# The head of a residual projection kernel: a weight loaded in three transfers, GpSimd adding the identity, products and a bias copy reordered

## The chip, the core and the metric

The kernel runs on one core of one Trainium2 chip. The metric is the device time of one execution in microseconds. A separate profiled execution gives the trace.

## What is computed

`x` is 128 x 128 x 512 in fp32, `cond` 128 x 512. With the 1024 x 512 `weight_matrix` cut into halves W_u and W_e:

```python
u = jax.nn.gelu(encoded_utterance @ W_proj + b_proj, approximate=False)
W_u, W_e = (weight_matrix[:D], weight_matrix[D:])
logits = (u @ W_u)[:, None, :] + jnp.einsum('bnd,dc->bnc', element_embeddings, W_e)
return x + logits
```

Here `encoded_utterance` is `cond` and `element_embeddings` is `x`. So the output is x (W_e + I) plus a bias row for each b, and the kernel computes it in that form.

## The kernel before

**The arithmetic.** Every fp32 operand is split into a high part (cast to the type fp32r) and a low part (the rest); a product is three matmul passes, high by high, high by low and low by high. W_e lies as `w_e[p, j, c]` in four slices j of 512 columns; the identity is added on a diagonal of each slice, then the slice is cast into `w_hi[j]` and the rest goes into `w_lo[j]`.

**The stages.** The first four of the 128 n ("direct" chunks 0 and 1, two n each) are multiplied plainly: TensorE transposes x (`flip`), ACT casts the high part (`direct_hi`), DVE makes the low part (`split_direct`), and TensorE multiplies (L688 for chunk 0, L726 to L728 for chunk 1). The other 124 n go in 31 quads of four n. In each quad the work is a 2 x 2 block scheme with seven products `m1` to `m7` instead of eight, 12 matmuls each (L743 to L747, `three_passes`), whose operands are blocks of x and their sums (`s1` to `s4`), and blocks of the weight and their sums (`t_sum`, `t_hi`, `t_lo`). DVE transposes the quad (`turn_up`, `turn_low`, L509) and forms `s1` (L552), `s3` (L558), `s2` (L564) and the low part of `s1` (L567); ACT casts the high parts (L391, L399), copies snapshots of partial sums between banks (L452, L461) and seeds banks with the bias (L424, L432); GpSimd makes the other low parts and `s4`. In a period k the products of quad k run while quad k+1 is prepared.

**The bias.** TensorE transposes `cond` (L673), multiplies with W_proj (L717), transposes again, ACT applies the GELU (L382), TensorE multiplies with W_u (L735) between the two halves of chunk 1's products, and DVE copies the sum to `bias` (L635) and makes `bias_step` (L637). ACT's `seed_a` (L424) waits for `bias_step`; `m1(0)` waits for the seed. `evacuate(c)` (L513) on DVE adds the bias to the direct chunks.

**Order.** Each engine has its own queue, in the order of the program, and semaphores between them. Around the change:

- SP issues all transfers: `load_direct(0)`, the two halves of W_e (L245, slices 0 and 1, then 2 and 3), `load_direct(1)`, `cond`, W_proj, b_proj, W_u, then the first quad in two halves (`load_first`, L232) and the next ones (L237).
- DVE: add the identity to slice 0, cast `w_hi[0]` (L608), `split_direct(0)`, add 1, `split_direct(1)`, add 2, add 3 (all L593), the four `split_w` (L602), four `t_sum`, `split_direct` of chunk 1, the transposes of quad 0, `sum_s1`, `sum_s2`, `split_s1`, `sum_s3`, bias copy, `bias_step`, `evacuate(0)`, `evacuate(1)`, the transposes of quad 1, and then, in `period(0)`, `combine_quad(1)`, which begins with `sum_s1(1)`.
- ACT: `direct_hi` of chunk 0, `w_hi[1]` to `w_hi[3]` (L364), chunk 1's, `t_hi` and `cond_t`, then for quad 0 `up`, `hi_s1`, `hi_a22`, `hi_s2`, `hi_s3`, `seed_a`, `seed_c`, `hi_s4`; in period 0 the bank copy L444, `seed_c(1)`, `up(1)`, `snap5` (L452), `seed_a(1)`, `hi_s1(1)`, `snap2` (L461).
- TensorE: six dummy matmuls on zeros, the transposes of chunk 0, eight more dummies (`WARM_ON`, L669), and then for each j: high products of slice j (two matmuls), low products of slice j, and the products with `w_lo[j-1]`; the transposes of chunk 1 stand at j = 2, that of `cond` at j = 3.
- GpSimd: the identity matrix, the four low parts of `t_sum` (L308), then quad work.

`m7(0)` waits for `snap2` (L461), `m5(0)` for `s1_lo` and `seed_c(0)`.

Of the kernel before, what the change touches and what calls it, by code (L numbers as in the profile page):

```python
# [8 lines left out]
ALU = mybir.AluOpType  # L9
# [6 lines left out]
HEAD_CHUNKS = 2  # L16
QUAD = 4
WARM_UP = 6
WARM_ON = 8


def build_cond_residual(nc, x, cond, weight_matrix, w_proj, b_proj, out):
# [18 lines left out]
    NJ = D // P  # L41
    NM = B // Q
    T = TILES_PER_CHUNK
# [13 lines left out]
    with ExitStack() as ctx:  # L57
# [3 lines left out]
        def sem(name):  # L61
            return ctx.enter_context(nc.semaphore(name))
# [76 lines left out]
        cond_loaded = sem("cond_loaded")  # L139
        w_proj_loaded = sem("w_proj_loaded")  # L140
        b_proj_loaded = sem("b_proj_loaded")
        w_e_loaded = [sem(f"w_e_loaded{n}") for n in range(2)]
        direct_loaded = [sem(f"direct_loaded{c}") for c in range(HEAD_CHUNKS)]
        direct_flipped = sem("direct_flipped")
        direct_hi_ready = sem("direct_hi_ready")
# [14 lines left out]
        bias_copied = sem("bias_copied")  # L160
        bias_ready = sem("bias_ready")
        w_diag_ready = sem("w_diag_ready")
        w_hi_ready = [sem(f"w_hi_ready{j}") for j in range(NJ)]
        w_lo_ready = [sem(f"w_lo_ready{j}") for j in range(NJ)]
        t_summed = sem("t_summed")
# [54 lines left out]
        def first_half(n):  # L220

            return quad_raw[0][:, n * T * TILE:(n + 1) * T * TILE].rearrange("p (m n w) -> p m n w", m=NM, n=T)

        def stores_before(k, p):

            return (k + p) * 8

        @block.sync
        def _(sp):
# [11 lines left out]
                sp.dma_start(direct[:, c * T:(c + 1) * T, :],  # L241
                             x[:, c * T:(c + 1) * T, :]).then_inc(direct_loaded[c], 16)

            def load_w_e(n):
                sp.dma_start(w_e[:, 2 * n:2 * n + 2, :], w_e_dram[:, 2 * n:2 * n + 2, :]).then_inc(w_e_loaded[n], 16)  # L245

            load_direct(0)
            for n in range(2):
                load_w_e(n)
            load_direct(1)  # L250
            sp.dma_start(cond_sb[:, :], cond).then_inc(cond_loaded, 16)
            sp.dma_start(w_proj_sb[:, :, :], w_proj_dram).then_inc(w_proj_loaded, 16)
# [31 lines left out]
            n = N - QUAD  # L284
# [14 lines left out]
        @block.gpsimd  # L299
        def _(pool):  # L300
            pool.memset(ident[:, :], 0.0).then_inc(ident_zeroed, 1)
            pool.wait_ge(ident_zeroed, 1)
            pool.affine_select(out=ident[:, :], in_=ident[:, :], compare_op=ALU.not_equal, fill=1.0,
                               base=0, pattern=[[-1, P]], channel_multiplier=1).then_inc(ident_ready, 1)

            def split_t(n):
                pool.wait_ge(t_hi_ready, n + 1)
                pool.tensor_tensor(t_lo[:, n, :, :], t_sum[:, n, :, :], t_hi[:, n, :, :].bitcast(F32),  # L308
                                   ALU.subtract).then_inc(t_lo_ready, 1)

            for n in range(4):
                split_t(n)

            def prepare(k, p, first=False):
                pool.wait_ge(up_hi, k + 1)
                pool.tensor_tensor(slot(lo[p], UP, 2), a_up[p], slot(hi[p], UP, 2).bitcast(F32),  # L316
                                   ALU.subtract).then_inc(up_lo, 1)

                def sum_s4():
                    pool.wait_ge(s2_ready, k + 1)  # L320
                    pool.tensor_tensor(s4[p], a12[p], s2[p], ALU.subtract).then_inc(s4_ready, 1)  # L321

                def split_s2():
                    pool.wait_ge(s2_hi, k + 1)
                    pool.tensor_tensor(slot(lo[p], S2), s2[p], slot(hi[p], S2).bitcast(F32),  # L325
                                       ALU.subtract).then_inc(s2_lo, 1)

                if first:
                    split_s2()
                    sum_s4()  # L330
                else:
                    sum_s4()
                    split_s2()
                pool.wait_ge(s4_hi, k + 1)
                pool.tensor_tensor(slot(lo[p], S4), s4[p], slot(hi[p], S4).bitcast(F32),  # L335
                                   ALU.subtract).then_inc(s4_lo, 1)
                pool.wait_ge(s3_hi, k + 1)
                pool.tensor_tensor(slot(lo[p], S3), s3[p], slot(hi[p], S3).bitcast(F32),
                                   ALU.subtract).then_inc(s3_lo, 1)
                pool.wait_ge(a22_hi, k + 1)  # L340
                pool.tensor_tensor(slot(lo[p], A22), a22[p], slot(hi[p], A22).bitcast(F32),  # L341
                                   ALU.subtract).then_inc(a22_lo, 1)

            prepare(0, 0, True)
            prepare(1, 1)
            with pool.Fori(1, QUADS // 2) as it:
                for p in range(2):
                    prepare(it * 2 + p, p)
            prepare(QUADS - 1, 0)

        @block.scalar
        def _(act):
# [7 lines left out]
            for n in range(T):  # L360
                direct_hi(n)
            for j in range(1, NJ):
                act.wait_ge(w_diag_ready, j + 1)
                act.copy(w_hi[:, j, :], w_e[:, j, :]).then_inc(w_hi_ready[j], 1)  # L364
            for n in range(T, HEAD):
                direct_hi(n)
# [140 lines left out]
        def _(dve):  # L507
# [79 lines left out]

            dve.memset(zeros[:, :], 0.0).then_inc(zeros_ready, 1)

            def add_identity(j):  # L590
                dve.wait_ge(w_e_loaded[j // 2], 16)
                diag = w_e[:, j, :].rearrange("p (a r) -> p a r", r=NJ)[:, :, j]
                dve.tensor_tensor(diag, diag, ident[:, :], ALU.add).then_inc(w_diag_ready, 1)  # L593

            def split_direct(n):
                dve.wait_ge(direct_hi_ready, n + 1)
                dve.tensor_tensor(x_lo[n // T][:, n % T, :, :], direct_psum[n % T],
# [5 lines left out]
                                  ALU.subtract).then_inc(w_lo_ready[j], 1)  # L603

            dve.wait_ge(ident_ready, 1)
            add_identity(0)
            dve.wait_ge(w_diag_ready, 1)
            dve.tensor_copy(w_hi[:, 0, :], w_e[:, 0, :]).then_inc(w_hi_ready[0], 1)  # L608
            split_direct(0)
            add_identity(1)  # L610
            split_direct(1)
            add_identity(2)
            add_identity(3)
            for j in range(NJ):
                split_w(j)

            b_of = w_e[:, :, :].rearrange("p (e j) (h c) -> p e h j c", e=2, h=2)
            b11, b12, b21, b22 = b_of[:, 0, 0], b_of[:, 0, 1], b_of[:, 1, 0], b_of[:, 1, 1]
            dve.wait_ge(w_diag_ready, NJ)
            dve.tensor_tensor(t_sum[:, 0, :, :], b12, b11, ALU.subtract).then_inc(t_summed, 1)  # L620
            dve.tensor_tensor(t_sum[:, 2, :, :], b22, b12, ALU.subtract).then_inc(t_summed, 1)
            dve.wait_ge(t_summed, 1)
# [5 lines left out]
            turn_up(0, 0, True)  # L628
            turn_low(0, 0, True)
            sum_s1(0, 0, True)  # L630
            sum_s2(0, 0)
            split_s1(0, 0)
            sum_s3(0, 0, True)
            dve.wait_ge(bias_summed, 1)
            dve.tensor_copy(bias[:, :], bias_psum).then_inc(bias_copied, 1)  # L635
            dve.wait_ge(bias_copied, 1)
            dve.tensor_tensor(bias_step[:, :], bias_psum[:, right], bias[:, left], ALU.subtract).then_inc(bias_ready, 1)  # L637
            evacuate(0)
            evacuate(1)
            turn_up(1, 1, True)  # L640
# [25 lines left out]
        def _(pe):  # L666
# [20 lines left out]
            def product(t, a, b, j, first=False, last=False):  # L687
                return pe.matmul(banks[0][:, t, :], a[:, t, j, :], b[:, j, :], start=first, stop=last)  # L688

            for j in range(NJ + 1):  # L690
                if j < NJ:
                    pe.wait_ge(w_hi_ready[j], 1)
                    for t in range(T):
                        if j == 0:
                            pe.wait_ge(direct_hi_ready, t + 1)
                        product(t, x_hi[0], w_hi, j, first=(j == 0))
                    for t in range(T):
                        if j == 0:
                            pe.wait_ge(direct_lo_ready, t + 1)
                        product(t, x_lo[0], w_hi, j)  # L700
# [149 lines left out]
```

## Time and profile before

| | us |
|---|---|
| median of 3 runs | 347.29 (346.6 to 347.96) |
| the profiled execution | 347.7 |
| its span, first to last instruction | 345.4 |
| TensorE busy with matmuls | 339.6 (98%) |
| DVE / ACT / GpSimd busy | 261.7 / 247.0 / 277.2 |

The span is what the instructions cover; 2.3 us of the execution's time lie around it. All rows below are from the profiled execution, and their times count from the start of its span. In a row, an engine's name with a q is its queue (SPq issues transfers). A matmul's duration includes its way through the array; start to start is what the next one waits.

### The profile page before, as it was taken

How to read it: one execution, taken by the hardware profiler on the slowest of the kernel's cores; microseconds unless marked ns; L12 is line 12 of the kernel's file. 1: busy time of each engine (PE TensorE's matmuls, PEld its weight loads, DVE VectorE, ACT ScalarE, POOL GpSimd, SP SyncE). 2: the span in 40 equal slices, each digit the busy share in tenths (PEclk: the TensorE clock that was granted, in tenths of full speed). 3: DMA queues.
4: the chain of work that ended last, by engine and by line, in shares of the span. 5: the costliest groups of instructions: out<-in, count | busy, mean ns of one | idle time of the engine just before them, and what ended most of it. 6: DMA issues, size and time to landing. Idle time of an engine off the chain costs nothing.

```text
span 345.4 us, 7856 instructions
## 1 busy us (share of the span) xinstructions
PE 339.6 (98%) x2706; PEld 328.7 (95%) x2706; DVE 261.7 (76%) x301; ACT 247.0 (72%) x424; POOL 277.2 (80%) x196
## 2 busy tenths in 40 slices
PE   7999999999999999999999999999999999999996
PEld 3758999999999999999999999999999999999996
DVE  2869977788777778877777897777789777778811
ACT  3646877877777787777778777777877777787741
POOL 0357998888989888898988889898888989888860
PEclk9999999999999999999999999999999999999999
DMA  7998697888799788879978887997887799788116
GB/s 257 331 180 236 123 238 201 221 194 204 176 228 241 195 219 196 198 180 229 237 200 218 195 197 178 232 233 202 219 197 197 175 235 237 197 209 210 83 56 228
DMA packets 72264, 70.64 MB, mean 205 GB/s; under 512 B 2880, under 2 KB 67392, under 8 KB 68032
## 3 DMA queue, kind: packets, MB, share of 16 engines
q1 hardware_dynamic: 72256, 70.53, 80.5%
q8 instruction: 5, 0.08, 0.1%
q14 instruction: 3, 0.02, 0.0%
HBM read 36.96 MB, written 33.55 MB: 204 GB/s over the span
## 4 chain that ended last, share of the span: by engine, by line
PE 89%; DVE 1%; ACT 0%; issue 0%
PE banks L743 30%; PE banks L747 29%; PE banks L745 29%; DVE work L509 1%; DVE banks L509 0%; DVE banks L552 0%; ACT snap_rows L461 0%; ACT y L504 0%; ACT hi L399 0%
## 5 line engine op out<-in xcount | busy, mean ns | idle before, releaser
L743 PE MATMUL banks<-t_hi,hi 128*128 128x256 f32 x496 | 140.5, 283 | 0.2 <-ACT snap_rows L461 0.2
L745 PE MATMUL banks<-t_lo,hi 128*128 128x256 f32 x496 | 140.4, 283 | 0.0
L747 PE MATMUL banks<-t_hi,lo 128*128 128x256 f32 x496 | 140.4, 283 | 0.0
L743 PE MATMUL banks<-w_hi,hi 128*128 128x256 f32 x372 | 105.3, 283 | 0.4 <-ACT banks L424 0.4
L745 PE MATMUL banks<-w_lo,hi 128*128 128x256 f32 x372 | 105.3, 283 | 0.0
L747 PE MATMUL banks<-w_hi,lo 128*128 128x256 f32 x372 | 105.3, 283 | 0.0
L509 DVE STREAM_TRANSPOSE work<-quad_raw 128x1024 f32<-128x1024 f32 (+1 forms) x62 | 100.7, 1624 | 3.6 <-DMA quad_raw<-in_x 3.6
L743 PEld LDWEIGHTS banks<-t_hi,hi 128*128 128x128 f32 x496 | 95.2, 192 | 0.6 <-issue 0.6
L747 PEld LDWEIGHTS banks<-t_hi,lo 128*128 128x128 f32 x496 | 95.2, 192 | 0.0
L745 PEld LDWEIGHTS banks<-t_lo,hi 128*128 128x128 f32 x496 | 95.2, 192 | 0.0
L316 POOL TENSOR_TENSOR lo<-work,hi 128x1024 fp32r<-128x1024 f32 x31 | 74.8, 2413 | 21.7 <-ACT hi L391 21.7
L399 ACT CAST hi<-work 128x512 fp32r<-128x512 f32 x124 | 71.0, 619 | 16.1 <-DVE work L564 8.4
L743 PEld LDWEIGHTS banks<-w_hi,hi 128*128 128x128 f32 x372 | 71.4, 192 | 0.8 <-issue 0.8
L747 PEld LDWEIGHTS banks<-w_hi,lo 128*128 128x128 f32 x372 | 71.4, 192 | 0.0
L745 PEld LDWEIGHTS banks<-w_lo,hi 128*128 128x128 f32 x372 | 71.4, 192 | 0.0
L321 POOL TENSOR_TENSOR work<-work 128x512 f32<-128x512 f32 x31 | 40.3, 1299 | 18.8 <-DVE work L564 18.8
L581 DVE TENSOR_TENSOR y<-banks,snap_rows 128x512 f32<-128x512 f32 x31 | 21.4, 691 | 36.2 <-PE banks L747 36.2
L444 ACT COPY banks<-banks 128x512 f32<-128x512 f32 x30 | 17.1, 570 | 44.4 <-PE banks L747 44.3
L586 DVE TENSOR_TENSOR y<-banks,snap_rows 128x512 f32<-128x512 f32 x31 | 21.4, 692 | 27.2 <-PE banks L747 27.2
L325 POOL TENSOR_TENSOR lo<-work,hi 128x512 fp32r<-128x512 f32 x31 | 40.5, 1305 | 1.4 <-ACT hi L399 1.4
L335 POOL TENSOR_TENSOR lo<-work,hi 128x512 fp32r<-128x512 f32 x31 | 40.4, 1302 | 1.4 <-ACT hi L399 1.4
L341 POOL TENSOR_TENSOR lo<-work,hi 128x512 fp32r<-128x512 f32 x31 | 40.6, 1310 | 0.0
(71 smaller groups left out, 401.7 us busy)
## 6 DMA issues: line engine op xcount, KB each, us to landing
out<-y SPq DMA_DIRECT2D x31, 1024.0 KB, 4.5
quad_raw<-in_x SPq DMA_DIRECT2D x120, 256.0 KB, 5.7
head_raw<-in_x SPq DMA_DIRECT2D x2, 512.0 KB, 5.7
w_e<-in_L_cond_weight_matrix SPq DMA_DIRECT2D x2, 512.0 KB, 6.2
w_proj_sb<-in_L_cond_W_proj SPq DMA_DIRECT2D x1, 1024.0 KB, 10.0
w_u<-in_L_cond_weight_matrix SPq DMA_DIRECT2D x1, 1024.0 KB, 12.3
quad_raw<-in_x SPq DMA_DIRECT2D x8, 128.0 KB, 9.5
out<-y SPq DMA_DIRECT2D x3, 256.0 KB, 2.1
```

Source lines behind the costliest of these rows:

```text
L316: pool.tensor_tensor(slot(lo[p], UP, 2), a_up[p], slot(hi[p], UP, 2).bitcast(F32), ALU.subtract).then_inc(up_lo, 1)
L321: pool.tensor_tensor(s4[p], a12[p], s2[p], ALU.subtract).then_inc(s4_ready, 1)
L325: pool.tensor_tensor(slot(lo[p], S2), s2[p], slot(hi[p], S2).bitcast(F32), ALU.subtract).then_inc(s2_lo, 1)
L335: pool.tensor_tensor(slot(lo[p], S4), s4[p], slot(hi[p], S4).bitcast(F32), ALU.subtract).then_inc(s4_lo, 1)
L341: pool.tensor_tensor(slot(lo[p], A22), a22[p], slot(hi[p], A22).bitcast(F32), ALU.subtract).then_inc(a22_lo, 1)
L399: act.copy(slot(hi[p], at), source).then_inc(done, 1)
L509: return dve.transpose(out_, in_)
L581: dve.tensor_tensor(y[p][:, upper, right], c_bank[p], snap2[p][:, :, :], ALU.add).then_inc(c12_out, 1)
L586: dve.tensor_tensor(y[p][:, lower, right], a_bank[p], snap5[p][:, :, :], ALU.add).then_inc(c22_out, 1)
L743: pe.matmul(psum[:, t, :], a_hi[:, 2 * j + t, :], b_hi[:, j, :], start=False, stop=False, skip_group_check=True)
L745: pe.matmul(psum[:, t, :], a_hi[:, 2 * j + t, :], b_lo[:, j, :], start=False, stop=False, skip_group_check=True)
L747: last = pe.matmul(psum[:, t, :], a_lo[:, 2 * j + t, :], b_hi[:, j, :], start=False, stop=(j == T - 1), skip_group_check=True)
```

## The change

W_e is loaded in three transfers instead of two: slice 0, slice 1, slices 2 and 3. DVE adds the identity to slice 0 only; GpSimd, behind its identity matrix, does so for slices 1 to 3. ACT's casts wait for GpSimd. TensorE runs six dummies instead of eight behind the first transposes, and then takes the high products of slice j+1 ahead of the low products of slice j. On DVE `sum_s3(0)` stands ahead of `sum_s2(0)`, and the bias copy and `bias_step` stand ahead of `split_s1(0)`.

```diff
-WARM_ON = 8
+WARM_ON = 6
...
-            def load_w_e(n):
-                sp.dma_start(w_e[:, 2 * n:2 * n + 2, :], w_e_dram[:, 2 * n:2 * n + 2, :]).then_inc(w_e_loaded[n], 16)
+            def load_w_e(n, js):
+                sp.dma_start(w_e[:, js, :], w_e_dram[:, js, :]).then_inc(w_e_loaded[n], 16)
 
             load_direct(0)
-            for n in range(2):
-                load_w_e(n)
+            load_w_e(0, slice(0, 1))
+            load_w_e(1, slice(1, 2))
+            load_w_e(2, slice(2, NJ))
             load_direct(1)
...
+            pool.wait_ge(ident_ready, 1)
+            for j in range(1, NJ):
+                pool.wait_ge(w_e_loaded[min(j, 2)], 16)
+                diag = diagonal(j)
+                pool.tensor_tensor(diag, diag, ident[:, :], ALU.add).then_inc(w_diag_ready, 1)
...
             for j in range(1, NJ):
-                act.wait_ge(w_diag_ready, j + 1)
+                act.wait_ge(w_diag_ready, j)
                 act.copy(w_hi[:, j, :], w_e[:, j, :]).then_inc(w_hi_ready[j], 1)
...
             dve.wait_ge(ident_ready, 1)
-            add_identity(0)
-            dve.wait_ge(w_diag_ready, 1)
+            dve.wait_ge(w_e_loaded[0], 16)
+            first_diag = diagonal(0)
+            dve.tensor_tensor(first_diag, first_diag, ident[:, :], ALU.add).then_inc(first_diag_ready, 1)
+            dve.wait_ge(first_diag_ready, 1)
             dve.tensor_copy(w_hi[:, 0, :], w_e[:, 0, :]).then_inc(w_hi_ready[0], 1)
             split_direct(0)
-            add_identity(1)
             split_direct(1)
-            add_identity(2)
-            add_identity(3)
             for j in range(NJ):
                 split_w(j)
...
             sum_s1(0, 0, True)
+            sum_s3(0, 0, True)
             sum_s2(0, 0)
-            split_s1(0, 0)
-            sum_s3(0, 0, True)
             dve.wait_ge(bias_summed, 1)
             dve.tensor_copy(bias[:, :], bias_psum).then_inc(bias_copied, 1)
             dve.wait_ge(bias_copied, 1)
             dve.tensor_tensor(bias_step[:, :], bias_psum[:, right], bias[:, left], ALU.subtract).then_inc(bias_ready, 1)
+            split_s1(0, 0)
             evacuate(0)
...
+            def high(j):
+                pe.wait_ge(w_hi_ready[j], 1)
+                for t in range(T):
+                    if j == 0:
+                        pe.wait_ge(direct_hi_ready, t + 1)
+                    product(t, x_hi[0], w_hi, j, first=(j == 0))
+
+
+            high(0)
             for j in range(NJ + 1):
+                if j + 1 < NJ:
+                    high(j + 1)
                 if j < NJ:
-                    pe.wait_ge(w_hi_ready[j], 1)
-                    for t in range(T):
-                        if j == 0:
-                            pe.wait_ge(direct_hi_ready, t + 1)
-                        product(t, x_hi[0], w_hi, j, first=(j == 0))
                     for t in range(T):
```

`diagonal(j)` is the view of slice j on which the identity is added, 128 elements a partition with a step of four.

## Rows read from the trace of the kernel before

**Rows 1.** Windows: busy time (x instructions) of each engine, PEclk, DMA share, GB/s.

```profile
36.70:342.70 306.00, 305.74 (x2544) 305.36 (x2544) 236.27 (x267) 227.84 (x390) 260.27 (x180) 1.00 0.80 201
```

**Rows 2.** Chain of waits, 18 to 37 us: start, us, what; one link.

```profile
35.96 0.60 ACT snap_rows L461
```

**Rows 3.** Timeline, TensorE, 22 to 37 us: start, us, line, tiles, count, idle before.

```profile
22.23 3.67 PE L735 MATMUL banks<-w_u,u_t 128*128 128x512 f32 x8
...
28.27 0.39 PE L728 MATMUL banks<-w_hi,lo 128*128 128x512 f32 x1
29.11 0.36 PE L743 MATMUL banks<-w_hi,hi 128*128 128x256 f32 x1 [0.45 <-ACT banks L424]
...
36.26 0.28 PE L747 MATMUL banks<-w_hi,lo 128*128 128x256 f32 x1
36.70 0.36 PE L743 MATMUL banks<-t_hi,hi 128*128 128x256 f32 x1 [0.16 <-ACT snap_rows L461]
```

**Rows 4.** Timeline, DVE, 21 to 31 us.

```profile
21.72 1.21 DVE L509 STREAM_TRANSPOSE banks<-quad_raw 128x512 f32<-128x512 f32 x1 [0.32 <-DMA quad_raw<-in_x]
...
24.05 0.70 DVE L552 TENSOR_TENSOR banks<-banks,work 128x512 f32<-128x512 f32 x1
25.40 0.69 DVE L564 TENSOR_TENSOR work<-banks,work 128x512 f32<-128x512 f32 x1 [0.65 <-ACT hi L399]
...
26.60 0.68 DVE L558 TENSOR_TENSOR work<-work,banks 128x512 f32<-128x512 f32 x1
27.20 0.68 DVE L635 COPY bias<-banks 128x512 f32<-128x512 f32 x1
27.92 0.42 DVE L637 TENSOR_TENSOR bias_step<-banks,bias 128x256 f32<-128x256 f32 x1
28.26 2.35 DVE L513 TENSOR_TENSOR y<-banks,bias 128x1024 f32<-128x1024 f32 x2
30.52 2.10 DVE L509 STREAM_TRANSPOSE work<-quad_raw 128x1024 f32<-128x1024 f32 x1
```

**Rows 5.** Timeline, ACT, 24 to 29 us: casts of s1 and s3, seed.

```profile
24.78 0.59 ACT L399 CAST hi<-banks 128x512 fp32r<-128x512 f32 x1 [1.76 <-DVE banks L552]
...
27.31 0.62 ACT L399 CAST hi<-work 128x512 fp32r<-128x512 f32 x1 [0.57 <-DVE work L558]
28.37 0.59 ACT L424 COPY banks<-bias 128x512 f32<-128x512 f32 x1 [0.44 <-DVE bias_step L637]
```

**Rows 6.** Tile w_e: issues (ns, first and last start), landing; then the page's GB/s slices.

```profile
L245 SPq DMA_DIRECT2D w_e<-in_L_cond_weight_matrix x2: 417/424/432, 1.2 to 1.7; - x2
...
DMA to landing us min/median/max: 5.3/6.2/7.0
...
GB/s 257 331 180 236 123 238 201 221 194 204 176 228 241 195 219 196 198 180 229 237 200 218 195 197 178 232 233 202 219 197 197 175 235 237 197 209 210 83 56 228
```

**Rows 7.** Timeline, all engines, 1 to 10 us.

```profile
1.20 2.74 PE L669 MATMUL banks<-zeros 128*128 128x512 bf16 x6 [1.20 <-DVE zeros L588]
...
5.47 1.89 PE L669 MATMUL banks<-zeros 128*128 128x512 bf16 x8
6.64 0.39 DVE L593 TENSOR_TENSOR w_e<-w_e,ident 128x128 f32<-128x128 f32 x1 [5.50 <-DMA w_e<-in_L_cond_weight_matrix]
7.06 0.43 DVE L608 CAST w_hi<-w_e 128x512 fp32r<-128x512 f32 x1
...
7.55 0.73 PE L688 MATMUL banks<-w_hi,hi 128*128 128x512 f32 x2 [0.18 <-DVE w_hi L608]
...
8.42 0.62 ACT L364 CAST w_hi<-w_e 128x512 fp32r<-128x512 f32 x1 [2.15 <-DVE w_e L593]
...
9.37 0.63 PE L688 MATMUL banks<-w_hi,hi 128*128 128x512 f32 x2
...
9.83 0.63 PE L688 MATMUL banks<-w_hi,lo 128*128 128x512 f32 x2
```

**Rows 8.** GpSimd: the first low part in the timeline; line L308's ns min/median/max.

```profile
14.04 1.62 POOL L308 TENSOR_TENSOR t_lo<-t_sum,t_hi 128x512 fp32r<-128x512 f32 x1 [12.55 <-ACT t_hi L370]
...
L308 POOL TENSOR_TENSOR t_lo<-t_sum,t_hi x4: 1265/1274/1622, 14.0 to 18.3; 128x512 fp32r<-128x512 f32 x4
```

More of the change, by code:

```diff
@@ L141, in build_cond_residual @@
         b_proj_loaded = sem("b_proj_loaded")
-        w_e_loaded = [sem(f"w_e_loaded{n}") for n in range(2)]
+        w_e_loaded = [sem(f"w_e_loaded{n}") for n in range(3)]
         direct_loaded = [sem(f"direct_loaded{c}") for c in range(HEAD_CHUNKS)]
@@ L162, in build_cond_residual @@
         w_diag_ready = sem("w_diag_ready")
+        first_diag_ready = sem("first_diag_ready")
         w_hi_ready = [sem(f"w_hi_ready{j}") for j in range(NJ)]
@@ L222, in first_half, with diagonal @@
             return quad_raw[0][:, n * T * TILE:(n + 1) * T * TILE].rearrange("p (m n w) -> p m n w", m=NM, n=T)
+        def diagonal(j):
+            return w_e[:, j, :].rearrange("p (a r) -> p a r", r=NJ)[:, :, j]
         def stores_before(k, p):
@@ L588, in _ @@
             dve.memset(zeros[:, :], 0.0).then_inc(zeros_ready, 1)
[L590 to L593, printed above, removed]
             def split_direct(n):
@@ L618, in _ @@
             b11, b12, b21, b22 = b_of[:, 0, 0], b_of[:, 0, 1], b_of[:, 1, 0], b_of[:, 1, 1]
-            dve.wait_ge(w_diag_ready, NJ)
+            dve.wait_ge(w_diag_ready, NJ - 1)
             dve.tensor_tensor(t_sum[:, 0, :, :], b12, b11, ALU.subtract).then_inc(t_summed, 1)
```

## The prediction

> **What bounds the kernel now.** The windows come first: from 36.7 us to 342.7 us TensorE is busy 305.74 of 306.00 us with 2,544 matmuls, its granted clock 1.00 [rows 1], one each 0.120 us. Nothing in the change touches these loops, so the change can only move the instant at which this dense stretch begins: the first matmul of `m7(0)`, at 36.70. Everything behind it moves with it, one for one, as long as no other engine falls behind by more than TensorE gains.
>
> Next, what releases that instant. TensorE's own rows [rows 3]: the last product of the head starts at 28.27; `m1(0)` starts at 29.11 after an idle time that ACT's seed L424 ends; then 60 matmuls (five products of 12) run without a hole, the last starting at 36.26. Left alone, `m7(0)` would start one pitch later, at 36.38. It starts at 36.70, and the releaser named is ACT's `snap_rows` L461, which is also the last link of the chain of waits [rows 2]. So TensorE is 0.32 us early there, and another chain arrives last. Its links: L461 stands on ACT behind `hi_s1(1)`, which needs `sum_s1(1)`, which needs both transposes of quad 1 on DVE, and those start at 30.52, straight behind the two `evacuate`s [rows 4]. From that 30.52 to `m7(0)` it is 6.18 us with no wait for TensorE in it. The reader should keep two numbers apart: what TensorE's arrival gains (call it the arrival, 36.38 now) and what the DVE chain gains (30.52 + 6.18 = 36.70 now). The later of the two sets the end.
>
> Upstream, the DVE chain starts with a transfer: the transpose of quad 0's lower half begins at 21.72 after idling for a DMA [rows 4]. Whatever DVE does earlier in the head is in the shadow of that landing.
>
> **Part 1, the order on DVE behind the transposes.** Before [rows 4, 5]: `sum_s1` 24.05; an idle 0.65 us for ACT's `hi_s1` (24.78 + 0.59); `sum_s2` 25.40; `split_s1`; `sum_s3` 26.60; bias copy 27.20; `bias_step` 27.92; the `evacuate`s 28.26 to 30.52, 1.13 each. Tensor operations of this size follow each other at 0.60 (26.60 to 27.20). After: `sum_s1` 24.05, `sum_s3` 24.65 in the former hole, `sum_s2` 25.40 as before, then bias copy at 26.0. Its sum is ready: the eight bias matmuls end at 22.23 + 3.67 = 25.90 [rows 3]. Then `bias_step` at 26.0 + 0.72 = 26.7, ready at 27.1; `split_s1` 27.05; `evacuate(0)` 27.65; `evacuate(1)` 28.8; transposes of quad 1 at 29.92. That is 30.52 less the 0.60 of `sum_s3`, which now lies in the hole. `evacuate(1)` needs the head's last product (28.27 + 0.39 = 28.66 [rows 3]), so it doesn't wait. `split_s1` comes 1.05 us later; `m5(0)` needs it only at about 30. The DVE chain then gives `m7(0)` = 29.92 + 6.18 = 36.10.
>
> The seed: ACT takes `hi_s3` at 26.7 now, since `s3` is ready early, ends at 27.3, and seeds from 27.3 to 27.9 instead of 28.37 to 28.96 [rows 5]. TensorE's last product leaves at 28.27 + 0.23 = 28.50. So `m1(0)` starts at about 28.5 instead of 29.11, and the arrival at `m7(0)` goes from 36.38 to about 35.8. `seed_c(0)` follows `evacuate(0)` and ends near 29.5, before `m5(0)` at 30.0. GpSimd's part for `s4` frees up as early: its ACT copy no longer stands behind the seed.
>
> Result so far: arrival 35.8, DVE chain 36.10. The chain decides: 0.60 us gained, and TensorE's idle time before `m7(0)` stays about 0.3.
>
> **Part 2, the weights in three transfers, GpSimd's adds, the high products of slice 1 first, six dummy matmuls instead of eight.** The first two slices came together, 5.3 us after an issue at 1.20, that is at 6.5; slices 2 and 3 came 7.0 after 1.65, at 8.65 [rows 6]. DVE started 0.14 behind the first. Alone, slice 0 should land about half a transfer earlier: (8.65 - 6.5)/2 = 1.1 us, at 5.4. With the add 0.42 and the copy 0.43 behind it (6.64 to 7.06 to 7.49 [rows 7]), `w_hi[0]` is ready at 6.4. TensorE is then in its dummies: eight ran from 5.47 with 1.89 us to the last one's end [rows 7], a pitch of 0.215, so six leave it free at 6.75. First products at 6.75 instead of 7.55: 0.8 us early.
>
> That lead is then lost, because the order is now high(0), high(1), low(0), high(2), and high(2) needs slices 2 and 3, which land when they did, 8.65. Chain: 8.65, 0.14 to the start, an add on GpSimd, ACT's cast 0.62 [rows 7], so high(2) starts at about 9.45 plus the add. For the add there is no row: nearest below is a quarter of GpSimd's 1.27 us for 512 columns, 0.32; nearest above is its whole first one, 1.62 [rows 8]; DVE takes 0.39 for it [rows 7]. I take 0.45, near the quarter, since the same work on 128 columns is one fourth. So high(2) starts at 9.9 to 9.95, with three groups done (high 0, high 1, low 0). Before, at 9.83, exactly these three were done too [rows 7]. TensorE is at the same point at the same time, late by 0.1. Behind it the same 18 products and 12 transposes follow in a similar order, and no other operand is late: `w_hi[3]` comes at 10.5 and is wanted at 11.3; DVE's `w_lo` come earlier than before since its adds are gone. The cost of the dummies and the early start is nothing either way. GpSimd's first add, of slice 1, is costed at 0.45 + 0.35 (the first tensor operation ran 1.62, the others 1.27); it leads to high(1) at about 8.1, in a hole.
>
> The arrival at `m7(0)` is thus 35.9, still before the DVE chain's 36.10. The bounds of the add put it at 35.8 to 37.3 (two adds in a row at 1.62: late by 1.5). The Trainium skill (SBUF — State Buffer, Who interferes with whom) says that a VectorE operation with two SBUF inputs and a GpSimd operation that reads SBUF exclude each other for a whole instruction. Here `split_w(1)` on DVE runs at about 8.2 to 8.9, beside the landing of slices 2 and 3; that would add 0.1 to 0.6 to the adds and, at its worst, bring the arrival to 36.5. No row shows it.
>
> **Part 3, one transfer more on SP's queue.** Everything behind it, `load_direct(1)`, the bias weights and all quads, is issued 0.42 us later [rows 6]. This lies under a full queue: the weights wait 5.3 to 7.0 us from issue to landing. What remains is the smaller packets. Between 0 and 0.42 I take 0.1, near 0 because of that backlog. It moves the landing on which the DVE chain hangs, so it counts in full: 36.10 + 0.1 = 36.2.
>
> **Sum.** 36.70 - 36.2 = 0.5 us. The profiled execution took 347.7 (span 345.4 and 2.3 around it), so it would take 347.2. It lies 0.4 above the median, 347.29; by the median the forecast is 346.8.
>
> **Rivals.**
> A, the transfers get faster. The weights' second 512 KB landed 2.15 us behind the first, 244 GB/s, where the page's second slice (8.6 to 17.3 us) moved 331 on average [rows 6]. At that pace 512 KB take 1.6 us; if smaller pieces win this 0.6 once, the quads land 0.6 earlier, the DVE chain gives 35.5, the arrival (weights early too, seed at 28.0) 35.3, and the gain is 1.2: 346.1. Against it: nothing in the rows says that the size of the pieces sets the pace, and the bytes and the queue are the same.
> B, the gain is eaten: quads land 0.42 late instead of 0.1, or the add on GpSimd takes about 1.1. Either makes `m7(0)` 36.5 to 36.7: 347.2.
> C, slower, the clock. TensorE would do six products (1.4 us) between 6.75 and 9.95 and idle 1.8. The dummies' pitch tells its levels: six took 2.74 us from 1.20 (0.43 each, 1.2 GHz), eight took 1.89 from 5.47 (0.215, 2.4 GHz) [rows 7]; so it rose within 4.3 us of the first. If the holes let it fall, up to 4.3 us of products run at half pace, 2.1 us lost; the arrival is 38.0, 1.3 later than now: 348.6. It decides once TensorE is late by over 0.9 (35.8 to 36.7). Against it: before, it idled some 1.1 us between 7.36 and 9.83 and the products behind kept 0.23.
> D, slower, GpSimd's first tensor operation needs something fetched. Now it stands behind a wait of 12.55 us, in which that could hide; with it at 6.6 it might not. By rows the first add could then end as late as 14.4, high(1) start at 15.4 instead of 9.37, and the total rise by up to 5.6: 352.9. For it: the first is 0.35 longer than the rest. Against it: no idle time but the wait for ACT's `t_hi` stands before it [rows 8]. The Trainium skill (GPSIMD Engine Reference, Instruction dispatch) says that the first call of a freshly loaded routine pays a load of about 6 us that no instruction shows; by that figure high(1) would start near 13.8 and the total would be about 351.3.
>
> **Chances.** Forecast 0.66, A 0.09, B 0.15, C 0.05, D 0.05. A measurement of this kernel can tell about 0.5% from no change, 1.7 us. Forecast, A, B and C (+1.3) lie within that, apart from noise at the edges; D does not. So faster 0.02, same 0.91, slower 0.07. The three runs of before spread over 1.36 us, so the range is the forecast with 0.9 below (A is in it) and 1.1 above (B and the dear end of the add): 345.9 to 347.9. C and D stay out.
>
> **What would show it.** In the trace after: `sum_s3` directly behind `sum_s1` and no DVE idle there; bias copy near 26.0; seed L424's counterpart near 27.3; `m1(0)` near 28.6; the transposes of quad 1 near 30.0; `m7(0)` near 36.2, released by `snap_rows` again. First product near 6.8, a hole before high(1) and one before high(2), which starts near 9.9. Wrong if high(2) comes after 10.8, if the transpose at 21.72 moves by over 0.3, if the product pitch behind 9.9 is over 0.23, or if `m7(0)` is released by TensorE itself.

## The result, and the profile after

The changed kernel takes 348.07 us (median of 19 executions, 347.2 to 349.94), the kernel before beside it 346.66 (19 executions). The ratio is 1.0037, with a 95% interval of 1.0026 to 1.0048: slower by some 1.3 us, where 0.5 us of gain was forecast. The change of 0.4% is less than the 0.5% of the chances, but the time lies above the range (347.9), and its sign is wrong.

Each execution also has the span of its instructions. The 112 executions of the kernel before that were run beside the experiments have a median span of 344.9, and a median time minus span of 1.86. After, the 19 have 345.7 and 2.31. So the loss has two parts, 0.7 to 0.8 us within the span and 0.45 outside it. And in 4 of the 19 the granted clock fell to 0.995 in the mean; these took 349.5 to 349.9, the other 15 took 347.2 to 348.3.

The trace taken with the result is one of those four (349.94 us, span 347.9). Its windows, columns as in [rows 1], and TensorE's timeline:

```profile
9.00:11.00 2.00, 0.41 (x2) 0.00 (x0) 0.49 (x1) 0.42 (x1) 0.97 (x2) 1.00 1.04 419
11.00:13.00 2.00, 1.75 (x4) 1.40 (x5) 1.77 (x3) 0.72 (x2) 0.01 (x1) 0.59 1.01 413
13.00:15.00 2.00, 2.00 (x7) 1.54 (x5) 1.97 (x4) 0.00 (x0) 0.00 (x0) 0.55 1.04 395
```

```profile
7.14 0.73 PE L694 MATMUL banks<-w_hi,hi 128*128 128x512 f32 x2
8.22 0.73 PE L694 MATMUL banks<-w_hi,hi 128*128 128x512 f32 x2 [0.34 <-ACT w_hi L376]
8.79 0.62 PE L694 MATMUL banks<-w_hi,lo 128*128 128x512 f32 x2
11.25 1.13 PE L694 MATMUL banks<-w_hi,hi 128*128 128x512 f32 x2 [1.83 <-ACT w_hi L376]
...
31.36 0.39 PE L740 MATMUL banks<-w_hi,lo 128*128 128x512 f32 x1
...
39.14 0.35 PE L755 MATMUL banks<-t_hi,hi 128*128 128x256 f32 x1 [0.20 <-ACT snap_rows L473]
```

The three groups high(0), high(1), low(0) are done as early as foretold. Then TensorE is idle for 1.83 us until `w_hi[2]` is there, the granted clock goes to 0.59 and 0.55 of full (between the levels 1.2 and 2.4 GHz: such a row holds some of each), and two products that took 0.46 us [rows 7] take 0.92 and 0.85 from start to start (11.25 to 12.17, 13.03 to 13.88). The row from 15 to 17 us is at 1.00 again. The head's last product starts at 31.36 instead of 28.27 [rows 3], `m7(0)` at 39.14 instead of 36.70.

This is the worst case. For a kernel's ordinary executions two later traces stand here, each with a span next to its kernel's median: e14 for the changed kernel (345.6, median 345.7) and e10 for the kernel before (344.8, median 344.9). First TensorE and DVE of e10, before:

```profile
9.91 0.63 PE L688 MATMUL banks<-w_hi,lo 128*128 128x512 f32 x2
10.37 0.63 PE L688 MATMUL banks<-w_lo,hi 128*128 128x512 f32 x2
10.84 0.63 PE L688 MATMUL banks<-w_hi,hi 128*128 128x512 f32 x2
...
28.34 0.39 PE L728 MATMUL banks<-w_hi,lo 128*128 128x512 f32 x1
...
36.11 0.36 PE L743 MATMUL banks<-t_hi,hi 128*128 128x256 f32 x1 [0.19 <-ACT snap_rows L461]
```

```profile
20.31 1.12 DVE L509 STREAM_TRANSPOSE banks<-quad_raw 128x512 f32<-128x512 f32 x1 [0.33 <-DMA quad_raw<-in_x]
...
26.02 0.69 DVE L635 COPY bias<-banks 128x512 f32<-128x512 f32 x1 [0.25 <-PE banks L735]
26.74 0.42 DVE L637 TENSOR_TENSOR bias_step<-banks,bias 128x256 f32<-128x256 f32 x1
27.08 1.22 DVE L513 TENSOR_TENSOR y<-banks,bias 128x1024 f32<-128x1024 f32 x1
28.76 1.23 DVE L513 TENSOR_TENSOR y<-banks,bias 128x1024 f32<-128x1024 f32 x1 [0.47 <-PE banks L728]
29.90 2.12 DVE L509 STREAM_TRANSPOSE work<-quad_raw 128x1024 f32<-128x1024 f32 x1
```

The reader should compare these with [rows 4]. There quad 0's lower half was turned at 21.72 and DVE never waited for TensorE. Here it is turned at 20.31, DVE has time left and waits for TensorE twice: 0.25 us ahead of the bias copy, and 0.47 ahead of `evacuate(1)`, which needs the head's last product. From that product to `m7(0)` it is 36.11 - 28.34 = 7.77 us without slack: 0.42 to `evacuate(1)`, 1.14 to the transposes of quad 1, and 6.21 from there (6.18 in the first trace).

Now e14, after:

```profile
7.08 0.73 PE L694 MATMUL banks<-w_hi,hi 128*128 128x512 f32 x2
8.16 0.74 PE L694 MATMUL banks<-w_hi,hi 128*128 128x512 f32 x2 [0.35 <-ACT w_hi L376]
8.73 0.62 PE L694 MATMUL banks<-w_hi,lo 128*128 128x512 f32 x2
10.50 0.74 PE L694 MATMUL banks<-w_hi,hi 128*128 128x512 f32 x2 [1.15 <-ACT w_hi L376]
...
29.07 0.39 PE L740 MATMUL banks<-w_hi,lo 128*128 128x512 f32 x1
...
36.84 0.35 PE L755 MATMUL banks<-t_hi,hi 128*128 128x256 f32 x1 [0.20 <-ACT snap_rows L473]
```

The last product is 0.73 us later than in e10, `m7(0)` is 0.73 later (and again 7.77 behind it), the span 0.8 longer. The hole of 1.15 us ahead of high(2) is where it comes from: with twelve products done, TensorE stands at 12.01 in e14 and at 11.30 in e10, 0.71 later.

### The profile page after: what moved, and what is told of

Read it like the earlier page. It is cut to its first block, busy times and chain, and to the rows that moved or that the text cites. A ratio compares the mean times of both kernels' runs of the same rounds, so it can differ in the third digit from the quotient of the medians.

```text
span 347.9 us, 7854 instructions
## 1 busy us (share of the span) xinstructions
PE 340.5 (98%) x2704; PEld 329.7 (95%) x2704; DVE 261.0 (75%) x298; ACT 246.7 (71%) x424; POOL 278.3 (80%) x199
## 4 chain that ended last, share of the span: by engine, by line
PE 88%; DVE 1%; ACT 0%; issue 0%
PE banks L755 29%; PE banks L759 29%; PE banks L757 29%; DVE work L521 0%; DVE banks L521 0%; DVE banks L564 0%; ACT snap_rows L473 0%; ACT y L516 0%; ACT hi L411 0%
## 6 DMA issues: line engine op xcount, KB each, us to landing
w_proj_sb<-in_L_cond_W_proj SPq DMA_DIRECT2D x1, 1024.0 KB, 10.8
```

## The experiments

Every kernel was run beside the kernel before on the same chip. "Span" is the median; "against before" is the mean span minus that of the executions of before beside it; fallen clock: executions with a mean granted clock of 0.995.

| kernel | executions | us | ratio (95%) | span | against before | time minus span | fallen clock |
|---|---|---|---|---|---|---|---|
| e1, after again | 12 | 348.12 | 1.0034 (1.0018 to 1.0049) | 345.8 | +0.66 | 2.34 | 2 |
| e2, loads only | 12 | 347.67 | 1.0011 (1.0000 to 1.0022) | 345.8 | +0.53 | 1.88 | 0 |
| e3, DVE order only | 12 | 346.92 | 1.0002 (0.9987 to 1.0017) | 345.1 | +0.03 | 1.86 | 0 |
| e4, after with two loads | 12 | 346.62 | 0.9999 (0.9985 to 1.0013) | 344.3 | -0.64 | 2.32 | 0 |
| e5, e4 with adds on DVE | 10 | 346.94 | 1.0003 (0.9993 to 1.0013) | 345.1 | +0.06 | 1.85 | 0 |
| e6, GpSimd adds only | 10 | 346.98 | 1.0008 (0.9994 to 1.0021) | 344.6 | -0.31 | 2.36 | 0 |
| e7, two loads, 2 KB rows | 10 | 347.49 | 1.0020 (1.0003 to 1.0036) | 345.7 | +0.64 | 1.85 | 1 |
| e8, three loads, 4 KB rows | 10 | 347.52 | 1.0020 (1.0007 to 1.0034) | 345.7 | +0.57 | 1.85 | 0 |
| e9, one GpSimd add | 10 | 347.03 | 0.9997 (0.9985 to 1.0008) | 345.1 | -0.09 | 1.88 | 0 |
| e11, after, old product order | 12 | 347.31 | 1.0007 (0.9997 to 1.0017) | 345.0 | +0.04 | 2.34 | 0 |
| e12, after, hole filled | 12 | 348.25 | 1.0036 (1.0024 to 1.0049) | 345.9 | +0.92 | 2.35 | 0 |
| e15, e4, old product order | 12 | 347.14 | 1.0016 (1.0005 to 1.0027) | 344.8 | +0.21 | 2.38 | 0 |

**What sets the end of the kernel before.** After e1 to e4 the theory was that TensorE's head, not the landing of the quads, is the bound in its usual executions. e10 is the kernel before, for one more trace.

> The kernel before, for a trace of one more of its executions. Theory H (in its usual executions the quads land early and TensorE's head sets the end: the head's last product, then evacuate(1), the transposes of quad 1 and the rest, 7.8 us to m7(0)): quad 0's lower half is transposed before 20.5, the bias copy waits for TensorE, m7(0) starts 7.8 us behind the last product, the span is 344.6 to 344.9. If this execution is like the first trace (quads at 21.7), the distance is 8.4 and the span 345.4.

It came out as theory H says; the rows stand above. It is one trace. The other runs that keep the two transfers of before (e3, e4, e5, e6, e9, e15) bear it out: quad 0's lower half is turned at 19.76 to 20.78 in all of them, and only the first trace of the kernel before has it at 21.72.

**The loads.** e1 is the changed kernel; e2 has only this edit:

```diff
...
-            for n in range(2):
-                load_w_e(n)
+            load_w_e(0, slice(0, 1))
+            load_w_e(1, slice(1, 2))
+            load_w_e(2, slice(2, NJ))
...
-                dve.wait_ge(w_e_loaded[j // 2], 16)
+                dve.wait_ge(w_e_loaded[min(j, 2)], 16)
```

> The changed kernel, unchanged, once more. In its first trace the quads landed 1.2 us late (DVE's transpose of quad 0's lower half at 22.94 instead of 21.72) and TensorE ran the products from 11.25 to about 15 us at half pace, with its granted clock at 0.55 to 0.59. Theory L (the loads: the third transfer, or its smaller packets, delays all that is loaded behind): the quads land 1.0 to 1.3 us late in every execution, also where the clock stays at 1.00, and the time is 1.2 to 1.5 us over before. Theory C (the clock: only the executions whose clock falls are slow): with the clock at 1.00 the quads land as before and the time is 0.5 below before.

> The kernel before with W_e in three transfers and nothing else. Theory L: the lower half of quad 0 is transposed at 22.7 to 23.0 and the time rises by 1.2 to 1.9 us, since the gain of the DVE order is missing. Theory C: no change, within 0.3 us, since TensorE's order and GpSimd are as before.

Neither expectation of e1 is met in full. Its trace has the lower half of quad 0 turned at 21.36. That is early against the first trace (21.72), but 1.05 us later than in e10 (20.31), and so with every kernel here that has a third transfer or short rows: in the nine traces of them (of the result, e1, e2, e7, e8, e11 to e14) it is turned at 21.22 to 22.94. So the late landing of theory L is there, but in e1's trace it doesn't set the end, since DVE waits 1.39 us for TensorE ahead of the bias copy. The trace is 1.1 us over e10 because the clock rose late: the six dummies took 2.76 us instead of 1.46, and the first product came at 8.57.

e2's extra is 0.5 to 0.8 us of span, less than expected, and it is the loads alone: GpSimd, TensorE's order and DVE's are those of before. In its trace slices 2 and 3 land at 2.1 + 7.4 = 9.5 us (e10: 1.65 + 6.3 = 7.95), and DVE, then TensorE, wait for them:

```profile
9.53 0.68 DVE L594 TENSOR_TENSOR w_e<-w_e,ident 128x128 f32<-128x128 f32 x2 [0.88 <-DMA w_e<-in_L_cond_weight_matrix]
...
10.85 0.73 PE L689 MATMUL banks<-w_lo,hi 128*128 128x512 f32 x2 [0.72 <-DVE w_lo L603]
...
28.91 0.39 PE L729 MATMUL banks<-w_hi,lo 128*128 128x512 f32 x1
...
37.02 0.36 PE L744 MATMUL banks<-t_hi,hi 128*128 128x256 f32 x1 [0.17 <-ACT snap_rows L462]
```

That makes the last product 0.57 us later than in e10. `m7(0)` is 0.91 later, 8.11 behind the last product and not 7.77, so here TensorE is not the bound and is 0.34 early. DVE is, from the landing of quad 0 on, without a wait for TensorE:

```profile
22.05 1.12 DVE L510 STREAM_TRANSPOSE banks<-quad_raw 128x512 f32<-128x512 f32 x1 [0.41 <-DMA quad_raw<-in_x]
...
27.51 0.68 DVE L636 COPY bias<-banks 128x512 f32<-128x512 f32 x1
...
30.83 2.10 DVE L510 STREAM_TRANSPOSE work<-quad_raw 128x1024 f32<-128x1024 f32 x1
```

This is the chain that the prediction read. It binds in the kernel before only when the quads land late, and the third transfer makes them land late.

Is it the number of transfers or their short rows? e7 keeps two transfers but takes slices 0 and 2, then 1 and 3:

```diff
-                sp.dma_start(w_e[:, 2 * n:2 * n + 2, :], w_e_dram[:, 2 * n:2 * n + 2, :]).then_inc(w_e_loaded[n], 16)
+                sp.dma_start(w_e[:, n:NJ:2, :], w_e_dram[:, n:NJ:2, :]).then_inc(w_e_loaded[n], 16)
...
-                dve.wait_ge(w_e_loaded[j // 2], 16)
+                dve.wait_ge(w_e_loaded[min(j, 1)], 16)
```

e8 takes three with rows of 4 KB, and DVE's adds wait for the halves that they need:

```diff
...
+            load_w_e(0, slice(0, P // 2), slice(0, 2))
+            load_w_e(1, slice(P // 2, P), slice(0, 2))
+            load_w_e(2, slice(0, P), slice(2, NJ))
```

> The kernel before with W_e in two transfers of 512 KB, but slices 0 and 2, then 1 and 3, so that each row moved is 2 KB instead of 4 KB. Theory S (the short rows are what made three transfers dear, 0.8 us of span): span 345.5 to 346.0, the second transfer lands over 1 us after 7.7. Theory N (the number of transfers): span as before, 344.8 to 345.2; DVE's add of slice 1 now waits for the second transfer, which it would reach at 7.8 anyway.

> The kernel before with W_e in three transfers whose rows are 4 KB: slices 0 and 1 of the first 64 partitions, of the other 64, then slices 2 and 3. Theory N: slices 2 and 3 land 0.8 to 1.2 us late, span 345.5 to 346.0. Theory S: span as before, 344.8 to 345.2.

Both are longer by about what e2 is, +0.64 (+0.47 without the one execution of e7 whose clock fell) and +0.57. So neither S nor N is right alone: each of the two brings the loss, and both together (e2) bring no more. The landings are late in both traces: the second transfer of e7 at 1.9 + 6.4 = 8.3 us, slices 2 and 3 of e8 at 2.5 + 6.6 = 9.1 (e10: 7.95), and quad 0's lower half is turned at 21.22 and 21.61. One thing is common to all three: SP spends longer on issuing. The two transfers of e7 take it 1.32 us, the three of e2 1.36 and those of e8 1.84, against 0.89 before, and the first quad is issued at 6.15, 5.83 and 5.99 against 4.84 in e10. A late issue of the quads is not enough as a cause, since the trace of the result has it at 5.40 and turns the quad at 22.94, while e15 has it at 5.41 and turns it at 20.78. Whether the later issue of what stands between or the shape of the transfers makes the quads late, no run separates, and e8's transfers also differ in covering 64 partitions. The traces of e7 and e8 have a late rise of the clock besides, so how much of their extra is the landing is open.

**DVE's order.** e3 makes the two edits on DVE alone.

> The kernel before with only the DVE order changed (sum_s3 ahead of sum_s2, the bias copy ahead of split_s1). By the prediction's part 1: the transposes of quad 1 start at 29.9, m7(0) at 36.1, the time falls by 0.6 us. Theory O (the order gains nothing, because another wait takes its place): no change, m7(0) at 36.7 with its release later than snap_rows of 0.6 earlier.

The gain of 0.6 is not there, and neither is theory O's `m7(0)` at 36.7. The trace tells why; DVE, then TensorE:

```profile
25.79 0.69 DVE L634 COPY bias<-banks 128x512 f32<-128x512 f32 x1 [1.71 <-PE banks L735]
26.51 0.42 DVE L636 TENSOR_TENSOR bias_step<-banks,bias 128x256 f32<-128x256 f32 x1
...
27.45 2.34 DVE L513 TENSOR_TENSOR y<-banks,bias 128x1024 f32<-128x1024 f32 x2
29.72 2.12 DVE L509 STREAM_TRANSPOSE work<-quad_raw 128x1024 f32<-128x1024 f32 x1
```

```profile
28.12 0.39 PE L728 MATMUL banks<-w_hi,lo 128*128 128x512 f32 x1
...
35.93 0.36 PE L743 MATMUL banks<-t_hi,hi 128*128 128x256 f32 x1 [0.23 <-ACT snap_rows L461]
```

Quad 0 was ready early, so the bias copy waits 1.71 us for TensorE; the hole that `sum_s3` filled only went into that wait. `m7(0)` starts 7.81 us behind the last product, as without the edit (7.77). The predicted start, 36.1, and the measured 35.93 agree by chance: e10 has 36.11 without the edit.

**The loads or the rest.** e4 is the changed kernel with W_e in the two transfers of before.

> The changed kernel with W_e in the two transfers of before. Theory L: the lower half of quad 0 is transposed at 21.7 again, high(2) starts near 10.0, and the time is 0.4 to 0.6 us below before. Theory C: TensorE still has a hole ahead of high(2); where the clock falls the time is 1.3 or more over before, in a share of the executions like that of the changed kernel (4 of 19).

The span falls by 0.6 to 0.7 (344.3). In its trace the lower half of quad 0 is turned at 20.24, high(2) follows at 9.29 without a hole, the last product starts at 27.73 and `m7(0)` at 35.50. So the edits other than the loads, taken together, shorten the head, and the three transfers cost 1.3 us of mean span in their company (+0.66 against -0.64; +0.40 against -0.64 without the two executions of e1 whose clock fell). But the time stays where it was and theory L's gain is missing, since time minus span is 2.32.

**Who lengthens the time outside the span.** e5 puts the adds of e4 back on DVE; e6 moves only the adds of before to GpSimd, the `pool.tensor_tensor` loop of the change:

> The two-transfer version of the changed kernel with the adds of slices 1 to 3 back on DVE. Of the changed kernel's 1.3 us, some 0.46 lie outside the span (time minus span 2.3 instead of 1.86; 1.86 too where only the loads or only the DVE order changed). Theory G (GpSimd's adds cost that 0.46): time minus span is 1.86 here. Theory T (TensorE's order or the number of dummies, the only other edits left): it stays 2.3. Span: with the adds on DVE the head loses what GpSimd took over, so 344.4 to 344.8 instead of 344.3.

> The kernel before with only the adds of slices 1 to 3 moved to GpSimd. Theory G: time minus span is 2.3, the span 0.3 to 0.6 shorter than before since DVE makes the low parts sooner, the sum 0 to 0.2 over before. Theory T: time minus span is 1.86 and the time is 0.3 to 0.6 below before.

Theory G holds in both. The span of e5 misses its expectation: it is 345.1, not 344.4 to 344.8, so with the adds on DVE the whole gain of e4 is gone (+0.06 against -0.64), while the adds on GpSimd by themselves (e6) bring 0.31. Counted by execution, time minus span is above 2.1 in 88 of the 91 executions that have three adds on GpSimd (10 of 10 in e6, where nothing else is changed), and in none of the 54 of e2, e3, e5, e7 and e8. The kernel before has it in 12 of 112. e9 leaves one add, slice 3's, on GpSimd:

> The kernel before with only slice 3's add moved to GpSimd. With all three adds there, time minus span rises from 1.86 to 2.36. If the price is fixed (some first use), time minus span is 2.3 to 2.4 here; if it is a price of each instruction, about 2.0.

Neither of the two prices: 6 of its 10 executions have 1.84 to 1.89 and 4 have 2.27 to 2.45. It is a step of about 0.5 us that an execution shows or doesn't. Three adds on GpSimd bring it nearly always. Whether one does is not shown, since of the 29 executions of the kernel before beside e9 nine have it too. Where in the execution it lies, no trace shows.

**The order of the products.** e11 is the changed kernel with `high(j)` back in its place, e15 the same with two transfers:

```diff
-            high(0)
             for j in range(NJ + 1):
-                if j + 1 < NJ:
-                    high(j + 1)
+                if j < NJ:
+                    high(j)
                 if j < NJ:
```

> The changed kernel with the products in the order of before (high(j+1) not ahead of low(j)). Theory Q (with slices 2 and 3 landing later, high(2) at the head of TensorE's queue holds up four products that could run, up to 0.94 us): median span 345.0 to 345.3 instead of 345.7, and no execution with a fallen clock. Theory P (the order doesn't matter, the loads alone do it): span 345.6 to 345.9 and the clock falls in some executions as it did in 6 of 31.

> The changed kernel with two transfers and the products in the order of before: the fourth corner beside three transfers with the new order (span 345.7), three with the old (345.0) and two with the new (344.3). Theory Q (the new order is dear only because slices 2 and 3 land late with three transfers): span 344.3 to 344.6, the order is worth nothing or up to 0.3 with two transfers, and 0.7 against with three. Theory R (the new order is dear by itself): span 343.6 to 343.9.

Median spans, and in brackets the mean against before:

| | old product order | new product order |
|---|---|---|
| two transfers | 344.8 (+0.21) | 344.3 (-0.64) |
| three transfers | 345.0 (+0.04) | 345.7 (+0.66) |

With two transfers the new order gains 0.5 to 0.85; with three it costs 0.6 to 0.7 (0.4 without the two executions of e1 whose clock fell). Theory Q holds, with a larger gain on its good side than expected, and e15's span of 344.8 lies above the 344.3 to 344.6 that it gave. In the new order TensorE wants slice 2 after 6 products, in the old one after 10; the four between are low(1) and the two with `w_lo[0]`, which could run and stand behind high(2). So beside the rest of the change each of the two edits by itself is harmless or good, and their sum is bad.

Two things this table leaves open. Beside the rest of the change the third transfer costs nothing in the old product order (+0.04 against +0.21), while alone it cost 0.53 (e2). One difference is DVE's new order, and an estimate says what it is worth where the quads are late. In e2, with the old order, 8.78 us pass from the turning of quad 0's lower half to the transposes of quad 1 (22.05 to 30.83). From e11's 22.66 this gives 31.44, and they start at 30.81, 0.6 us sooner; from e14's 22.19 it gives 30.97 against 30.65. No run takes only this edit back. And the number of dummies was never changed alone: e15 differs from e6 by it and by DVE's order (+0.03 in e3), and lies at +0.21 against -0.31, on another chip.

**The hole and the clock.** e12 puts four dummies ahead of high(2): `if j == 1: warm(4)`.

> The changed kernel with four dummy matmuls on zeros (0.86 us) between low(0) and high(2), where TensorE stood idle for 1.83 us in the execution whose clock fell. If the hole makes the clock fall, no execution is above 347 us of span, where 6 of 31 were; the others are 345.7 to 346.2, since the dummies cost up to 0.4 where the hole is short. If the clock falls for another reason, about 2 of 12 still show 0.995 and 347.2.

None of the 12 has a fallen clock, and none of the 12 of e11, whose order leaves no such hole; of the 33 executions of the changed kernel, 6 have one. That speaks for the hole as the cause, but doesn't show it: with 12 executions, a rate of 6 in 33 would show none about once in ten times, and one of the 10 executions of e7 has a fallen clock (0.995, span 347.3) with the product order of before. The dummies cost more than they save (+0.92).

**A usual execution of the changed kernel.** Two more traces of it:

> The changed kernel for a trace of a usual execution, with the clock not fallen. Theory Q: a hole of TensorE ahead of high(2), which starts at 10.3 to 10.7, the last product of the head at 28.9 to 29.2, span 345.5 to 345.9. If instead the usual execution is late by a clock that rises late, as in the second trace (dummies at 0.42 each, first product at 8.57), there is no hole ahead of high(2).

> A second look at the same: the same two outcomes as for the look before; both together say which of them is the usual one.

e14, shown above, is as theory Q says. e13 (span 346.1) is the other outcome: the dummies run from 6.57 at 0.42 each, the first product comes at 8.78, and high(2) stands at 11.18 without a hole. So the late rise is a second way in which executions differ. It is in the traces of e5, e7, e8, e11 and e15 as well, whose transposes of chunk 0 take 1.95 us where the other traces have 1.20 to 1.59, so it doesn't belong to the change. Of the three traces of the changed kernel in which the clock didn't fall, two have it (e1 and e13, spans 345.9 and 346.1) and one has the hole (e14, 345.6). By its span e14 is the ordinary one, but three traces don't settle which outcome is the commoner.

e14 also shows what slows the adds. GpSimd, its durations in ns, and DVE beside it:

```profile
L316 POOL TENSOR_TENSOR w_e<-w_e,ident x3: 517/521/1032, 6.9 to 9.8; 128x128 f32<-128x128 f32 x3
```

```profile
8.76 1.51 POOL L316 TENSOR_TENSOR w_e<-w_e,ident 128x128 f32<-128x128 f32 x2 [1.31 <-DMA w_e<-in_L_cond_weight_matrix]
...
8.14 1.28 DVE L609 TENSOR_TENSOR w_lo<-w_e,w_hi 128x512 fp32r<-128x512 f32 x2
```

The add of slice 2 starts at 8.76 and takes 1.03 us, not 0.52, beside `split_w(1)` on DVE, which runs to 9.42. In e1 and e13 one add takes 1.05 and 0.92 beside a `split_w`; in the trace of the result, where DVE was idle from 9.5 to 11.2, all three take 0.52.

## Why the prediction was wrong, point by point

**What sets the end.** That nothing behind `m7(0)` changes, one for one, was right: between e10 and e14 `m7(0)` moves by 0.73 and the span by 0.8. The step that failed is the next one: that the landing of quad 0 releases the DVE chain and TensorE is early by 0.32. It was read rightly from the trace, but that execution was not a usual one. It took 347.7 us beside a median of 347.29, and of 346.8 over the 112 later ones; I noted the 0.4 and took it off the time, instead of asking whether it sat in the very chain that I was reading. In e10 the quads land 1.4 us earlier and TensorE is the bound. The cushion that the prediction granted to TensorE, 0.9 us from 35.8 to 36.7, is not there: in e10 and e14 `m7(0)` stands 7.77 us behind the last product, and what the head loses, the span loses.

**Part 1, DVE's order.** The 0.60 was the main term of the sum, and on the kernel before it is 0 (e3: +0.03). The mechanism exists only where the quads land late. In the changed kernel they do, so there the edit is worth some 0.3 to 0.6 us by the estimate above (not tested): it keeps a loss away instead of bringing a gain.

**Part 2, "slices 2 and 3 land when they did, 8.65".** They land at 2.1 + 6.6 = 8.7 in e14, so the number is right there, and the comparison is wrong: in e10 they land at 7.95. So in e14 they are 0.75 later than in a usual execution of the kernel before. In the trace of the result they land at 9.9, 1.95 later than in e10. The comparison of progress at high(2) had the same flaw one step on: it showed that TensorE had done three groups at 9.83 in both cases, but the kernel before wants slice 2 only at 10.8, one microsecond and four products later. What should have been compared is the time at which each order first needs the late operand.

**The add on GpSimd.** Estimated 0.45, measured 0.52 alone and 0.9 to 1.05 beside `split_w`. The Trainium skill (SBUF — State Buffer, Who interferes with whom) says that a VectorE instruction with two SBUF inputs contends with a GpSimd instruction that reads SBUF. The trace of e14 agrees: 0.51 us more, beside a `split_w` that ran on for 0.66 us. The prediction named it, priced it at 0.1 to 0.6, and left it out of the sum; it is 0.5 and lies on the path to high(2). It is the greater part of what puts high(2) at 10.50 instead of 9.9. The first add has no extra (0.52), against the 0.35 allowed.

**Outside the span.** The prediction carried 2.3 us around the span through as a constant. It is 1.86 in most executions of the kernel before and 2.3 in those with three adds on GpSimd (e5 and e6 show that it is the adds), 0.45 of the 1.3 us. No part of the prediction asked whether an edit could change it.

**Part 3.** One more transfer and shorter rows were priced at 0.1, up to 0.42, as the delay of the quads' landing. Quad 0's lower half is turned 1.05 to 2.6 us later than in e10 in the traces of the changed kernel (21.36 to 22.94 against 20.31). In span they bring 0.5 to 0.8 alone (e2) and 1.3 with the rest of the change (e1 against e4): the term that was mis-sized most.

**The rivals.** A and B's time (347.2) did not occur; B's mechanism, a dear add and a late landing, did, and would have given the right sign had TensorE been taken as the bound. C, the fallen clock, occurs in 6 of 33 executions and costs 1.5 us in them (349.5 against 348.0); its chance of 0.05 was too low, and the hole it rested on was in the prediction's own sum. D did not happen: the adds start as soon as their slices land. The range ended at 347.9 because the largest known costs were set off against the cushion of 0.9; without it they give 348 and more.

**What it cannot say.** Why short rows and a third transfer each delay the landings is open, as is what the six dummies do by themselves, and whether the hole alone makes the clock fall. No version here beats the kernel before beyond noise: e4 has the shortest span, and gives it back outside (0.9999).

## What to carry to other kernels

Before a chain is read as the bound, ask how the profiled execution stands to the median, and whether its excess could lie in that chain: a transfer that lands 1.4 us late in one execution made a wait look like a law. When work is pulled ahead in an in-order queue, compare when the old and the new order first need the operand that lands last, and what ready work now stands behind it. Two edits should be priced together where one delays an operand and the other asks for it sooner: beside the rest of this change the new order alone gained up to 0.85 us, the third transfer alone cost nothing, and with both the span is 0.66 longer than before. And an edit that is worth nothing on the kernel before can still matter beside another edit that moves the bound.

## What the runs showed of the hardware that was not expected

- Time minus span has two values, about 1.86 and 2.3 us. With three small adds on GpSimd at 7 to 10 us 88 of 91 executions have the larger; of the kernels without any, 0 of 54 have it, and 12 of 112 of the kernel before. With one add it is 4 of 10, beside 9 of 29 of the kernel before.
- The instant at which TensorE's clock rises differs between executions of one kernel: behind the same six dummies from 1.20 us, the next dummies ran at 0.215 us each from 5.48 in e14 and at 0.42 from 6.57 to beyond 8 in e13; 0.5 us of span lies between the two.
- Splitting 512 KB of a 1 MB load in two, or taking it in rows of 2 KB instead of 4 KB, costs some 0.6 us of span each (e7, e8), though DMA moves the same bytes. Between 6 and 8 us it moved 278 to 365 GB/s in the nine traces with a third transfer or short rows and 390 to 418 in the eight without. The row of e14, then that of e10:

```profile
6.00:8.00 2.00, 1.67 (x7) 0.50 (x5) 1.80 (x4) 0.79 (x2) 0.52 (x1) 1.00 0.98 308
```

```profile
6.00:8.00 2.00, 2.00 (x10) 0.89 (x8) 1.25 (x3) 0.58 (x2) 0.00 (x0) 1.00 1.02 418
```
